# First token group of the last feed-forward block taken in two halves of 256 rows, late weight panels rounded on ScalarE

## The chip, the cores and the metric

The kernel runs on one core of a Trainium2 chip. The metric is the device time of one execution in microseconds (us), the median of three runs for the kernel before: 541.84 us (539.55 to 542.74). Lower is better.

## What is computed

Two batches of 1024 tokens of width 256 go through four residual blocks, all in float32: attention against 64 context rows per batch, a mixture of 16 experts of which each token takes two, a linear mix with a constant row of the context, and a feed-forward block with ternary weights. The change lies between the second and the fourth. Cut to that:

```
def _L1_xattn_ref(x1, x2, W, b):
    part1 = jnp.einsum('bld,ed->ble', x1, W1)
    part2 = jnp.einsum('bld,ed->be', x2, W2) / x2.shape[1]
    return part1 + part2[:, None, :] + b

def _L1_ffn_ref(x, w1_w, w1_s, w2_w, w2_s, h1_w, h1_s, h2_w, h2_s, w3_w, w3_s):
    h = jax.nn.silu(_tlin(x, w1_w, w1_s)) * _tlin(x, w2_w, w2_s)
    h = jax.nn.gelu(_tlin(h, h1_w, h1_s), approximate=False)
    h = jax.nn.gelu(_tlin(h, h2_w, h2_s), approximate=False)
    return _tlin(h, w3_w, w3_s)
...
x = x + tanh(g_ffn[0])   * L0_ffn(layernorm(x), ...)      # experts
x = x + tanh(g_xattn[1]) * L1_xattn(layernorm(x), ctx)    # linear mix
x = x + tanh(g_ffn[1])   * L1_ffn(layernorm(x), ...)      # 256 -> 1024 -> 1024 -> 1024 -> 256
```

## The kernel before

The 2048 tokens stand in X as 16 tiles of 128 rows, in NG = 4 groups of TG = 4 tiles (GN = 512 rows). Each engine has its own program, written out by hand in one order; engines meet only at semaphores. A matrix product in full float32 precision is made of products of the fp32r type: each operand is split in a rounded part (xTh, Ah, Bh, suffix h) and the rest (xTl, Al, Bl, suffix l). The ternary weights are exact in fp32r, so they need only the rounding copy from Wraw to Wr, in 44 panels of 512 columns; every product with them is two matmuls, one with the h part and one with the l part.

After the last of 47 expert blocks (NBLK) GpSimd (POOL) gathers the two expert rows of each token from ys_dram, `gather_rows` (L482 to L492): eight indirect DMAs for a group, into xn and y2. Then a group goes through this chain:

- VectorE (DVE) `x2` (L846): per tile two SCALAR_TENSOR_TENSOR into X (L850, L853), bn_stats (L859), bn_aggr (L861), at the end the variance into veps (L865).
- TensorE (PE) `T3` (L1411): two transposes a tile of X into banks 6 and 7. ScalarE (ACT) `high` (L1119) copies them to xTh, DVE `low3` (L867) makes xTl.
- POOL `root` (L439): rstd = veps ** -0.5; `add_row` (L494): adds the context row to the group's X.
- PE `part1` (L1422): three matmuls of 256 columns, twice, for each tile. DVE `x3` (L875): adds the product times rstd to X, then `statistics` (L544) for the fourth layer norm. POOL `root` again. DVE `normalise4` (L887): xn, one TENSOR_SCALAR a tile (L893). PE `T4` (L1432), ACT `high` (L1122), DVE `low4` (L896).
- `ffn` on all four engines (DVE L912, ACT L1124, PE L1439). Layer 1 has eight steps m (FK = 8): eight matmuls of 512 columns into two banks (L1468, L1471), banks alternating with m, so that step m waits for the DVE product of step m - 2 (semaphores f_h). ACT: Silu (L1134), then the copy to Ah (L1138). DVE: the product with the second bank (L917), then Al (L921). The layers h1 and h2 have eight steps of 16 matmuls of 512 columns (L1502, L1503) and Gelu on ACT (L1146); the last layer has 64 matmuls pairs of 256 columns (L1533, L1534).

For the groups 1 to 3 the chain is woven into the ffn of the group before, and hides there. For group 0 nothing is left to weave it into: it stands alone between the experts and the first ffn. PE fills that time with `keep_clock` (L1175), matmuls on the identity whose result nobody reads:

```
            eng.wait_ge(b_ye, NBLK)
            keep_clock(bank[0], 40)
            T3(0)
            keep_clock(bank[0], 8)
            part1(0)
            keep_clock(bank[0], 12)
            T4(0)
            keep_clock(bank[0], 4)
```

The panels are rounded by three engines: 0 to 7 on DVE among the expert blocks, 8 to 27 on ACT after them (L1116), and the last 16 (LATE) on POOL between its second root and the gathers of group 1 (L515). PE waits for the counters act_pan and pool_late before it uses a panel in group 0.

## Time and profile before

| | |
|---|---|
| median of 3 runs | 541.84 us (539.55 to 542.74) |
| the profiled execution | 541.48 us |
| its span in the profile | 539.7 us |
| mean granted TensorE clock | 0.961 of full |
| busy share: PE, DVE, ACT, POOL | 94%, 59%, 38%, 27% |

Times in the rows are in us from the start of the span. The profiled execution took 1.8 us more than its span, and 0.4 us less than the median. A matmul's duration includes the way through the array, so the step from one start to the next is the throughput; a matmul on float32 operands is recorded as two pieces. "Idle before" and an arrow name what ended the wait of that engine.

### The profile page before, as it was taken

The numbers are of one execution on the slowest core, as the hardware profiler recorded it, in microseconds if no ns is written. First come the engines' busy times: TensorE is split into PE (matmuls) and PEld (weight loads), VectorE is DVE, ScalarE is ACT, GpSimd is POOL, SyncE is SP. The second block draws the span as 40 slices with busy tenths as digits, with TensorE's granted clock in tenths as the row PEclk, the third lists the DMA queues.
The fourth block names the chain that finished last, engine by engine and source line by source line (L and its number), as shares of the span: only waits on it lengthen the run. The fifth ranks groups of instructions, "written<-read, shape, count | busy, mean of one in ns | idle before, by whom it ended". The sixth has DMA issues, their size and how long they took to land.

```text
span 539.7 us, 8120 instructions
## 1 busy us (share of the span) xinstructions
PE 509.5 (94%) x2866; PEld 435.1 (81%) x2866; DVE 320.6 (59%) x849; ACT 204.2 (38%) x453; POOL 148.0 (27%) x141
## 2 busy tenths in 40 slices
PE   8899998999998889999999999999999999999993
PEld 7778697888887767888897888897788888788883
DVE  3978956776652656874637775635686634644432
ACT  3666515666668035221226212224422123522120
POOL 1845336555525394110125020107011101000000
PEclk9778689999999799999999999999999999999998
DMA  8934214999883732231005031004122002022001
GB/s 291 310 101 135 67 41 118 316 302 311 223 144 91 279 105 65 57 80 40 1 1 156 21 97 60 0 2 136 40 78 72 7 1 79 1 79 78 21 1 44
DMA packets 33921, 54.63 MB, mean 101 GB/s; under 512 B 4081, under 2 KB 17905, under 8 KB 33874
## 3 DMA queue, kind: packets, MB, share of 16 engines
q1 hardware_dynamic: 29264, 43.06, 25.1%
q0 software_dynamic: 3792, 10.36, 8.2%
q10 hardware_dynamic: 818, 0.61, 0.4%
q8 instruction: 26, 0.43, 0.3%
q14 instruction: 21, 0.17, 0.1%
HBM read 43.66 MB, written 10.35 MB: 100 GB/s over the span
## 4 chain that ended last, share of the span: by engine, by line
PE 86%; DMA 4%; DVE 4%; issue 2%; POOL 2%; ACT 1%; SPq 0%; POOLq 0%; DVEq 0%
PE bank L1502 22%; PE bank L1503 22%; PE bank L1471 5%; PE bank L1468 5%; PE bank L1178 4%; PE bank L1171 4%; PE bank L1173 3%; PE bank L1172 3%; PE bank L1534 3%; PE bank L1533 3%; DMA xg<-xb_dram,perm 3%; PE bank L1361 2%; PE bank L1255 2%; PE bank L1231 2%; PE bank L1379 1%
## 5 line engine op out<-in xcount | busy, mean ns | idle before, releaser
L1146 ACT ACTIVATE sg<-bank,colv 128x512 f32<-128x512 f32 x64 | 44.1, 690 | 188.8 <-PE bank L1503 188.8
L1502 PE MATMUL bank<-Ah,Wr 128*128 128x512 f32 x256 | 100.2, 392 | 0.2 <-DVE sg L917 0.2
L1502 PE MATMUL bank<-Bh,Wr 128*128 128x512 f32 x256 | 99.9, 390 | 0.0
L1503 PE MATMUL bank<-Bl,Wr 128*128 128x512 f32 x256 | 99.7, 389 | 0.0
L1503 PE MATMUL bank<-Al,Wr 128*128 128x512 f32 x256 | 99.7, 389 | 0.0
L478 POOL DMA_INDIRECT xg<-xb_dram,perm x47 | 46.6, 991 | 42.9 <-PE bank L1361 21.3
L1502 PEld LDWEIGHTS bank<-Ah,Wr 128*128 128x128 f32 x256 | 48.0, 188 | 11.5 <-DVE sg L917 1.0
L1502 PEld LDWEIGHTS bank<-Bh,Wr 128*128 128x128 f32 x256 | 48.1, 188 | 9.8
L1503 PEld LDWEIGHTS bank<-Bl,Wr 128*128 128x128 f32 x256 | 48.1, 188 | 9.8
L1503 PEld LDWEIGHTS bank<-Al,Wr 128*128 128x128 f32 x256 | 48.1, 188 | 9.7
L930 DVE CAST Ah<-sg 128x512 fp32r<-128x512 f32 x32 | 13.6, 426 | 63.0 <-ACT sg L1146 63.0
L1471 PE MATMUL bank<-xTl,Wr 128*128 128x512 f32 x128 | 50.4, 394 | 0.2 <-DVE xTl L899 0.2
L1468 PE MATMUL bank<-xTh,Wr 128*128 128x512 f32 x128 | 50.4, 394 | 0.0
L441 POOL TENSOR_TENSOR rstd<-veps,mhalf 128x4 f32<-128x4 f32 x8 | 10.5, 1310 | 120.5 <-DVE veps L566 66.5
L917 DVE SCALAR_TENSOR_TENSOR sg<-bank,colv,sg 128x512 f32<-128x512 f32 x32 | 24.0, 751 | 24.2 <-ACT sg L1134 20.6
L1134 ACT ACTIVATE sg<-bank,colv 128x512 f32<-128x512 f32 x32 | 22.1, 689 | 42.1 <-PE bank L1471 37.7
L1178 PE MATMUL bank<-ident 128*128 128x128 f32 x252 | 35.3, 303 | 0.5 <-ACT yb L1100 0.5
L1178 PEld LDWEIGHTS bank<-ident 128*128 128x128 f32 x252 | 33.8, 216 | 2.2 <-issue 1.3
L930 DVE CAST Bh<-sg 128x512 fp32r<-128x512 f32 x32 | 13.6, 426 | 35.3 <-ACT sg L1146 35.3
L1171 PE MATMUL bank<-EL,bxh 128*128 x94 | 30.8, 327 | 1.2 <-DVE bxl L806 0.7
L1534 PE MATMUL bank<-Wr,Al 128*128 128x256 f32 x128 | 30.9, 283 | 0.0
L1533 PE MATMUL bank<-Wr,Ah 128*128 128x256 f32 x128 | 30.9, 283 | 0.0
(215 smaller groups left out, 1039.7 us busy)
## 6 DMA issues: line engine op xcount, KB each, us to landing
Wraw<-panels SPq DMA_DIRECT2D x22, 512.0 KB
stage<-panels SPq DMA_DIRECT2D x44, 256.0 KB
ES<-experts SPq DMA_DIRECT2D x16, 384.0 KB, 6.1
ys_dram<-yb SPq DMA_DIRECT2D x47, 128.0 KB
xb_dram<-xb SPq DMA_DIRECT2D x4, 512.0 KB, 4.0
X<-x SPq DMA_DIRECT2D x3, 512.0 KB, 7.6
out<-outb SPq DMA_DIRECT2D x3, 512.0 KB
xg<-xb_dram,perm POOLq DMA_INDIRECT x47
```

What stands on the lines that cost most here:

```text
L478: eng.indirect_dma_start(out=xg[:, i % 4, :], out_offset=None, in_=xb_dram, in_offset=bass.IndirectOffsetOnAxis(ap=perm[:, i:i + 1], axis= ...
L917: eng.scalar_tensor_tensor(sg[:, m % 3, :], bank[2 * (m % 2) + 1][:, :], colv[:, C_S2 + m:C_S2 + m + 1], sg[:, m % 3, :], ALU.mult, ALU.mu ...
L930: own(eng.tensor_copy(h[0][:, m, :], sg[:, r, :]))
L1146: eng.activation(sg[:, (8 * layer + m) % 3, :], bank[m % 4][:, :], ACT.Gelu, scale=colv[:, c + m:c + m + 1]).then_inc(f_act[m], 1)
L1171: mm(dst, lhs[0], rhs[1], start=first, stop=False)
L1178: mm(dst[:, 0:P], ident[:, :], ident[:, :], start=True, stop=True)
L1468: mm(dst, w[:, u, k, :], xTh[:, k, :], start=k == 0, stop=False)
L1471: ins = mm(dst, w[:, u, k, :], xTl[:, k, :], start=False, stop=k == DK - 1 and not general)
L1502: mm(bank[m % 4][:, :], Wr[:, base:base + P], h[0][:, k, :], start=k == 0, stop=False)
L1503: ins = mm(bank[m % 4][:, :], Wr[:, base:base + P], h[1][:, k, :], start=False, stop=k == FK - 1 and not general)
L1533: mm(dst, hA[0][:, k, j * P:(j + 1) * P], w, start=k == 0, stop=False)
L1534: ins = mm(dst, hA[1][:, k, j * P:(j + 1) * P], w, start=False, stop=k == FK - 1)
```

## The change

Group 0 goes through the chain, and through layer 1 of its ffn, in two halves of 256 rows (HN): `early` is rows 0 to 255, `late` rows 256 to 511. Every engine gets half versions of the functions (`root_half`, `add_row_half`, `x2_row`, `variance_half`, `low_half`, `x3_half`, `normalise4_half`, `high_half`, `T3_half`, `part1_half`, `T4_half`) and a function `early_layer1`: layer 1 for the early rows, with the second half's steps at fixed places in it. `ffn(0)` then makes layer 1 for the late rows only (`ts`), and the layers h1, h2 and w3 as before on 512 rows. The half versions use banks 4 and 5 for the product of part 1. Both halves of layer 1 have all eight steps, with matmuls of 256 columns: 128 matmuls where there were 64. The last 16 panels go from POOL to ACT: two after each Gelu of layer h1 of group 0. `keep_clock` in this place has 50 matmuls in all where it had 64. The groups 1 to 3 keep their code; only the semaphore counts are shifted by one (`passed(g)` = g + 2). The branch for weights that aren't exact is not taken.

```
@@ gpsimd @@
             gather_rows(0)
-            root(2, 0)
-            add_row(0)
-            root(3, 0)
-            for w in range(NPAN - LATE, NPAN):
-                raw_there(eng, w)
-                to, raw = panel(w)
-                eng.tensor_copy(to, raw).then_inc(pool_late, 1)
+            root_half(2, 0)
+            add_row_half(0)
+            root_half(3, 0)
+            root_half(2, 1)
+            add_row_half(1)
+            root_half(3, 1)
             for g in range(NG - 1):
                 gather_rows(g + 1)
@@ vector @@
+            def early_layer1():
+                for m in range(FK + 1):
+                    if m < FK:
+                        eng.wait_ge(e_act, m + 1)
+                        eng.scalar_tensor_tensor(sg[:, m % 3, early], bank[2 * (m % 2) + 1][:, early],
+                                                 colv[:, C_S2 + m:C_S2 + m + 1], sg[:, m % 3, early],
+                                                 ALU.mult, ALU.mult).then_inc(e_h, 1)
+                    if m > 0:
+                        eng.wait_ge(e_hh, m)
+                        eng.tensor_tensor(hA[1][:, m - 1, early], sg[:, (m - 1) % 3, early],
+                                          hA[0][:, m - 1, early].bitcast(F32), ALU.subtract).then_inc(e_hl, 1)
+                    if m == 1:
+                        x3_half(1)
+                    if m == 3:
+                        normalise4_half(1)
+                    if m == 6:
+                        low_half(1, n_h4, n_l4)
...
-            x2(0)
-            low3(0)
-            x3(0)
-            normalise4(0)
-            low4(0)
+            for j in range(2):
+                x2_row(0, j)
+            variance_half(2, 0)
+            low_half(0, n_h3, n_l3)
+            x2_row(0, 2)
+            x3_half(0)
+            x2_row(0, 3)
+            variance_half(2, 1)
+            normalise4_half(0)
+            low_half(1, n_h3, n_l3)
+            low_half(0, n_h4, n_l4)
+            early_layer1()
@@ scalar @@
+            def early_layer1():
+                for m in range(FK + 1):
+                    if m < FK:
+                        eng.wait_ge(e_pe, m + 1)
+                        if m >= 3:
+                            eng.wait_ge(e_hl, m - 2)
+                        eng.activation(sg[:, m % 3, early], bank[2 * (m % 2)][:, early], ACT.Silu,
+                                       scale=colv[:, C_S1 + m:C_S1 + m + 1]).then_inc(e_act, 1)
+                    if m > 0:
+                        eng.wait_ge(e_h, m)
+                        eng.activation(hA[0][:, m - 1, early], sg[:, (m - 1) % 3, early], ACT.Copy).then_inc(e_hh, 1)
+                    if m == 6:
+                        high_half(1, n_T4, n_h4)
...
+                        if g == 0 and layer == 1:
+                            w = NPAN - LATE + LATE // FK * m
+                            round_panels(w, w + LATE // FK)
@@ tensor @@
+            def early_layer1():
+                for m in range(FK):
+                    if m == 0:
+                        eng.wait_ge(n_h4, 1)
+                        eng.wait_ge(n_l4, 1)
+                    if m >= 2:
+                        eng.wait_ge(e_h, m - 1)
+                    eng.wait_ge(dve_pan, m + 1)
...
+                    if m == 0:
+                        part1_half(1)
+                    if m == 5:
+                        T4_half(1)
...
+                    elif g == 0:
+                        eng.wait_ge(n_h4, DK)
+                        eng.wait_ge(e_h, FK - 1 + m)
...
-            keep_clock(bank[0], 40)
-            T3(0)
-            keep_clock(bank[0], 8)
-            part1(0)
-            keep_clock(bank[0], 12)
-            T4(0)
-            keep_clock(bank[0], 4)
+            keep_clock(bank[0], 30)
+            T3_half(0)
+            keep_clock(bank[0], 3)
+            part1_half(0)
+            T3_half(1)
+            keep_clock(bank[0], 6)
+            T4_half(0)
+            keep_clock(bank[0], 3)
+            early_layer1()
```

How the instructions stand on VectorE, from the third tile of group 0 (L850 before, L867 now) to the first step of layer 1. Before, all of the chain comes ahead of the ffn's first product (L917):

```order
L850 SCALAR_TENSOR_TENSOR X<-xn,wtop,X 128x256
L853 SCALAR_TENSOR_TENSOR X<-y_60,wtop,X 128x256
L859 BN_STATS stats<-X 128x6
L861 BN_AGGR mv<-stats 128x2
L865 TENSOR_SCALAR veps<-mv 128x4
L870 TENSOR_TENSOR xTl<-bank,xTh 128x512 x2
L882 SCALAR_TENSOR_TENSOR X<-bank,rstd,X 128x256 x2
```

Now, from `low_half(0, n_h3, n_l3)` on:

```order
L892 TENSOR_TENSOR xTl<-bank,xTh 128x2x256
L867 SCALAR_TENSOR_TENSOR X<-xn,wtop,X 128x256
L870 SCALAR_TENSOR_TENSOR X<-y_60,wtop,X 128x256
L873 BN_STATS stats<-X 128x6
L875 BN_AGGR mv<-stats 128x2
L900 SCALAR_TENSOR_TENSOR X<-bank,rstd,X 128x256 x2
L904 BN_STATS stats<-X 128x6 x2
L907 BN_AGGR mv<-stats 128x2 x2
L887 TENSOR_SCALAR veps<-mv 128x2
L867 SCALAR_TENSOR_TENSOR X<-xn,wtop,X 128x256
```

The third tile now stands behind the first half's xTl, and the fourth tile behind the first half's `x3_half(0)`.

Further on in the same queue, the first steps of `early_layer1` (L964 is its product, L969 its Al):

```order
L964 SCALAR_TENSOR_TENSOR sg<-bank,colv,sg 128x256 x2
L969 TENSOR_TENSOR Al<-sg,Ah 128x256
L900 SCALAR_TENSOR_TENSOR X<-bank,rstd,X 128x256 x2
L904 BN_STATS stats<-X 128x6 x2
L907 BN_AGGR mv<-stats 128x2 x2
L887 TENSOR_SCALAR veps<-mv 128x2
L964 SCALAR_TENSOR_TENSOR sg<-bank,colv,sg 128x256
```

The product of step 2 stands behind the second half's `x3_half(1)`.

TensorE at the same place, from the first filler matmuls (L1281 is `keep_clock`) to the second half of part 1's first rows (L1520 is `T3_half`, L1537 `T4_half`):

```order
L1275 MATMUL bank<-W1h,xTl 128x256
L1276 MATMUL bank<-W1h,xTh 128x256
L1520 MATMUL bank<-ident,X 128x128 x4
L1281 MATMUL bank<-ident 128x128 x6
L1537 MATMUL bank<-ident,xn 128x128 x4
L1281 MATMUL bank<-ident 128x128 x3
L1553 MATMUL bank<-xTh,Wr 128x256
```

The transposes of the tiles 2 and 3 (four at L1520) now lie between the first half of part 1 and the first half of T4, with no filler between the two tiles.

## Rows read from the trace of the kernel before

**Rows 1.** The page: busy time, and the chain that ended last, by engine.
```profile
PE 509.5 (94%) x2866; PEld 435.1 (81%) x2866; DVE 320.6 (59%) x849; ACT 204.2 (38%) x453; POOL 148.0 (27%) x141
...
PE 86%; DMA 4%; DVE 4%; issue 2%; POOL 2%; ACT 1%; SPq 0%; POOLq 0%; DVEq 0%
```

**Rows 2.** Busy time by stretch: PE, PEld, DVE, ACT, POOL, then granted clock, DMA.
```profile
173.00:176.40 3.40, 0.80 (x6) 0.32 (x4) 2.04 (x6) 1.28 (x3) 2.52 (x3) 1.00 0.40 117
176.40:183.30 6.90, 4.96 (x22) 4.56 (x23) 4.04 (x10) 1.08 (x2) 3.35 (x2) 0.51 0.64 211
183.30:193.50 10.20, 7.96 (x64) 7.05 (x62) 6.19 (x18) 0.66 (x2) 4.80 (x9) 1.00 0.91 333
193.50:209.00 15.50, 15.34 (x67) 11.61 (x67) 9.72 (x15) 8.37 (x14) 13.20 (x18) 1.00 0.18 52
```

**Rows 3.** TensorE in order of time: start, us, what, idle time before it.
```profile
163.94 9.20 PE L1178 MATMUL bank<-ident 128*128 128x128 f32 x80 [0.47 <-ACT yb L1100]
...
179.51 3.62 PE L1178 MATMUL bank<-ident 128*128 128x128 f32 x16
...
183.45 0.28 PE L1171 MATMUL bank<-W1l,xTh 128*128 128x256 f32 x1
...
185.84 0.28 PE L1173 MATMUL bank<-W1h,xTh 128*128 128x256 f32 x1
...
193.58 0.47 PE L1468 MATMUL bank<-xTh,Wr 128*128 128x512 f32 x1
...
208.98 0.40 PE L1502 MATMUL bank<-Ah,Wr 128*128 128x512 f32 x1
```

**Rows 4.** VectorE in order of time, 174 to 200 us.
```profile
174.22 0.48 DVE L850 SCALAR_TENSOR_TENSOR X<-xn,wtop,X 128x256 f32<-128x256 f32 x1 [2.01 <-issue]
...
177.97 0.48 DVE L850 SCALAR_TENSOR_TENSOR X<-xn,wtop,X 128x256 f32<-128x256 f32 x1 [0.49 <-DMA y<-ys_dram,slots]
...
180.38 1.29 DVE L870 TENSOR_TENSOR xTl<-bank,xTh 128x512 fp32r<-128x512 f32 x2 [0.53 <-ACT xTh L1122]
184.82 0.88 DVE L882 SCALAR_TENSOR_TENSOR X<-bank,rstd,X 128x256 f32<-128x256 f32 x2 [3.15 <-PE bank L1173]
...
188.47 0.17 DVE L566 TENSOR_SCALAR veps<-mv 128x4 f32<-128x4 f32 x1
189.77 2.54 DVE L893 TENSOR_SCALAR xn<-X,mv,rstd 128x256 f32<-128x256 f32 x4 [1.13 <-POOL rstd L441]
...
197.00 0.75 DVE L917 SCALAR_TENSOR_TENSOR sg<-bank,colv,sg 128x512 f32<-128x512 f32 x1 [2.24 <-ACT sg L1134]
...
199.49 0.68 DVE L921 TENSOR_TENSOR Al<-sg,Ah 128x512 fp32r<-128x512 f32 x1
```

**Rows 5.** GpSimd in order of time, 179 to 199 us.
```profile
179.94 1.04 POOL L441 TENSOR_TENSOR rstd<-veps,mhalf 128x4 f32<-128x4 f32 x1 [3.81 <-DVE veps L865]
180.98 2.35 POOL L498 TENSOR_TENSOR X<-X,crow 128x1024 f32<-128x1024 f32 x1
...
189.71 9.24 POOL L515 CAST Wr<-Wraw 128x512 fp32r<-128x512 f32 x16
```

**Rows 6.** ScalarE in order of time.
```profile
159.10 0.39 ACT L1084 ACTIVATE bxh<-bank 128x256 fp32r<-128x256 f32 x1
...
163.79 10.49 ACT L1116 ACTIVATE Wr<-Wraw 128x512 fp32r<-128x512 f32 x20
...
196.28 0.69 ACT L1134 ACTIVATE sg<-bank,colv 128x512 f32<-128x512 f32 x1 [2.35 <-PE bank L1471]
...
216.52 0.69 ACT L1146 ACTIVATE sg<-bank,colv 128x512 f32<-128x512 f32 x1 [2.95 <-PE bank L1503]
```

**Rows 7.** VectorE in order of time, inside the ffn of group 0.
```profile
235.84 2.77 DVE L932 TENSOR_TENSOR Bl<-sg,Bh 128x512 fp32r<-128x512 f32 x1
...
259.92 1.38 DVE L893 TENSOR_SCALAR xn<-X,mv,rstd 128x256 f32<-128x256 f32 x4
```

**Rows 8.** GpSimd in order of time, inside the ffn of group 0.
```profile
235.58 2.48 POOL L498 TENSOR_TENSOR X<-X,crow 128x1024 f32<-128x1024 f32 x1 [9.17 <-PE bank L1418]
```

More of the change, by code:

```diff
@@ L311, in panel, with passed @@
             return Wr[:, w * PANEL:(w + 1) * PANEL], Wraw[:, w * PANEL:(w + 1) * PANEL]
+        HN = GN // 2
+        early, late = slice(0, HN), slice(HN, GN)
+        def passed(g):
+            return g + 2
         def tiles(g):
@@ new lines, in low_half, with x3_half @@
+            def low_half(h, ready, done_sem):
+                eng.wait_ge(ready, h + 1)
+                ts = slice(h * HN, (h + 1) * HN)
+                eng.tensor_tensor(xTl[:, :, ts], bank[6 + h][:, :].rearrange("p (k t) -> p k t", k=DK),
+                                  xTh[:, :, ts].bitcast(F32), ALU.subtract).then_inc(done_sem, 1)
+            def x3_half(h):
+                eng.wait_ge(n_row, h + 1)
+                eng.wait_ge(ln_rstd[2], h + 1)
+                eng.wait_ge(n_p1, h + 1)
+                for j in range(2 * h, 2 * h + 2):
+                    own(eng.scalar_tensor_tensor(tiles(0)(j), bank[4 + h][:, (j % 2) * D:(j % 2 + 1) * D],
+                                                 rstd[:, 2, j:j + 1], tiles(0)(j), ALU.mult, ALU.add))
+                own.done()
+                for j in range(2 * h, 2 * h + 2):
+                    own(eng.bn_stats(stats[:, j, :], tiles(0)(j)))
+                own.done()
+                for j in range(2 * h, 2 * h + 2):
+                    own(eng.bn_aggr(mv[:, 3, j, :], stats[:, j, :]))
+                variance_half(3, h)
@@ L867, in low3, with normalise4_half @@
+            def normalise4_half(h):
+                eng.wait_ge(ln_rstd[3], h + 1)
+                for j in range(2 * h, 2 * h + 2):
+                    eng.tensor_scalar(xn[:, j, :], tiles(0)(j), mv[:, 3, j, 0:1], rstd[:, 3, j:j + 1],
+                                      ALU.subtract, ALU.mult).then_inc(n_xn, 1)
             def low3(g):
@@ L1408, in _, with T3_half @@
                     load_offsets(i + 2)
+            def T3_half(h):
+                for j in range(2 * h, 2 * h + 2):
+                    if j == 1:
+                        keep_clock(bank[0], 8)
+                    eng.wait_ge(n_x2, j + 1)
+                    for k in range(DK):
+                        ins = eng.transpose(bank[6 + h][:, k * HN + (j % 2) * P:k * HN + (j % 2 + 1) * P],
+                                            tiles(0)(j)[:, k * P:(k + 1) * P], ident[:, :])
+                ins.then_inc(n_T, 1)
@@ new lines, in early_layer1 @@
+            def early_layer1():
[6 more added lines that the diff above has]
+                    eng.wait_ge(dve_pan, m + 1)
+                    w = Wr[:, m * PANEL:(m + 1) * PANEL].rearrange("p (u k n) -> p u k n", u=2, k=DK)
+                    for u in range(2):
+                        dst = bank[2 * (m % 2) + u][:, early]
+                        for k in range(DK):
+                            mm(dst, w[:, u, k, :], xTh[:, k, early], start=k == 0, stop=False)
+                            ins = mm(dst, w[:, u, k, :], xTl[:, k, early], start=False, stop=k == DK - 1)
+                    ins.then_inc(e_pe, 1)
+                    if m == 0:
+                        part1_half(1)
+                    if m == 5:
+                        T4_half(1)
```

140 lines of the change are left out of this document (85 added, 55 removed).

## The prediction

> **What bounds the kernel now.** The page comes first: PE is busy for 94% of the span and makes up 86% of the chain that ended last [rows 1]. That is an average over two kinds of stage, so I took the time apart by stretch. From 193.5 us on PE is busy all the time [rows 2], and it stays so to the end but for the last store: what happens after layer 1 of group 0 has begun costs exactly PE's own work. Between the end of the experts and that point PE does little that is wanted. It runs fillers from 163.94, and the first matmul of layer 1 starts at 193.58 [rows 3]. These 29.6 us are a chain through all engines: gathers, x2, transposes, xTl, part 1, x3, root, normalise, transposes, xTl. The reader should see two marks there: 193.58, where layer 1 starts, and 208.98, where layer h1 starts [rows 3]. From 208.98 on, the two kernels have the same PE work, so **the whole question is whether the first matmul of h1 comes before or after 208.98**. I walk the new order through, engine by engine, with durations from the rows.
>
> **Prices.** A matmul of 256 columns takes 0.12 us from start to start: 20 steps between 183.45 and 185.84 [rows 3]. A step of layer 1 for half the rows (eight of them) is 0.96, where the whole one is (208.98 - 193.58) / 8 = 1.92. So PE pays nothing or 0.2 us for splitting; the first step before had short waits in it. ACT on 256 columns takes 0.39 against 0.69 on 512 [rows 6]. DVE on 256 columns from PSUM or from SBUF takes 0.48, on 512 0.75 [rows 4]; for Al on 256 columns I take 0.41, between half of 0.68 and 0.48. A half of xTl or xTh is one instruction of 512 elements, 0.65 [rows 4]. From the last matmul's start to the next engine's is 0.3 us, and 0.03 to 0.1 for the other hand-overs. POOL's root is 1.04 whatever its size (bounds 0.5 and 1.4), the added row for half the group half of 2.35, 1.2 [rows 5].
>
> **Until layer 1 starts for the early rows.** The rows of tile 1 are on DVE at 174.22 [rows 4], and the gathers are untouched. X is there at 175.2, transposed at 175.8, xTh at 176.4, xTl at 177.1; part 1 (12 matmuls) runs from 177.2 to 178.8. POOL's root starts at 176.25, its added row runs from 177.3 to 178.5. DVE takes tile 2 from 177.06. Its two operations read two SBUF tiles each, and the second would start at 177.58, under POOL's addition. What that costs no row shows for this operation; the nearest one is the TENSOR_TENSOR at 235.84, 2.77 us where the same operation on Al takes 0.68 [rows 4]: it ends just after POOL's addition of 235.58 [rows 7, 8]. So an operation with two SBUF inputs has waited for POOL there. Bounds: nothing, or the rest of the addition, 1.15 us; I take the latter. Tile 2 is then through at 179.8, `x3_half(0)` takes 2.3 us (for four tiles it was 184.82 to 188.64 [rows 4]), tile 3 1.75, its variance 0.17: 183.9. Normalising two tiles takes 0.7: the four took 2.54 while POOL was casting panels [rows 4, 5], and 1.38 where it wasn't [rows 7]. That is the one sure gain of taking the casts off POOL, 0.6 us a half. `keep_clock(6)` after the transposes of tile 3 (183.1 to 183.4) ends at 184.85, so T4 starts then; xTh at 186.3, xTl at 187.0: **layer 1 starts at 187.05, 6.5 us before 193.58**.
>
> The Trainium skill (SBUF — State Buffer, Who interferes with whom) states that a VectorE instruction with two SBUF inputs and a GpSimd one that reads SBUF exclude each other for a whole instruction. That covers SCALAR_TENSOR_TENSOR too, which no row here shows; by it the 1.15 us are owed, without it the start is 186.05.
>
> **The early layer.** Its 64 matmuls are 7.7 us, part 1 of the late rows 1.44, T4 0.6. PE would be done in 9.7. DVE isn't: eight products and eight Al are 7.1 us, and x3 (2.3), normalise (0.7) and xTl (0.65) of the late rows stand among them in its queue, 10.8 in all, before any wait. Steps 0 to 3 of PE run from 187.05 to 192.6. The product of step 2 stands behind `x3_half(1)`, which ends at 194.0, so PE's step 4 waits for it until 194.55: **2.0 us idle**. Steps 4 and 5, T4 and steps 6 and 7 then run to 199.0. The late rows' xTh stands on ACT behind Silu 6 and copy 5, their xTl on DVE behind the product of step 6 and an Al: ready at 200.2, so PE idles 1.1 us more and starts the late half at 200.3. Early part: 13.2 us where PE's work is 9.7.
>
> **The late half.** Two steps in flight, as before, but with half the work against the same hand-overs: from the end of step m to the start of m + 2 it takes 0.17 (way through the array) + 0.04 + 0.39 + 0.04 + 0.48 + 0.07 = 1.19 us, and step m + 1 covers 0.96 of it. So two steps cost 2.15 where the 512-row form had all of this covered (1.92 us against some 1.7). Eight steps: 8.4 us, to 208.7. The Al of step 7 is needed only at the fifteenth matmul of h1, 3.2 us later, and is there.
>
> **Sum of the steps:** 208.7 against 208.98, -0.3 us. Layer 1 starts 6.5 us earlier, but where it took 15.4 us in one piece it now takes 13.2 + 8.4 = 21.6, 6.2 more: 2.0 is chain work of the late rows that PE does inside it, 3.1 are the two holes, and the rest are the longer steps.
>
> **The clock.** Before, PE ran at 1.2 GHz from 176.4 to 183.3 (granted 0.51) and at 2.4 GHz afterwards [rows 2]; it had been busy for 0.80 of the 3.4 us ahead of the fall. It cost little, for what PE did then was filler (16 pieces in 3.62 us against 80 in 9.20 [rows 3]). Now the holes are: 1.4 us at 173.9, 3.6 us between the transposes of tiles 2 and 3, 2.0 in the early layer. A fall behind the second doubles the 2.2 us of PE work between tile 3's transposes and layer 1, and perhaps a step or two. I put in 0.9 us, between nothing (fall at the old place) and 2.2 (a stretch as long as the old one that begins at 183.3).
>
> **The panels.** ACT's 16 copies are 0.52 each [rows 6], 1.05 after each Gelu of h1, where ACT idles 2.95 [rows 6]. The panels landed before POOL cast them, by 198.95 [rows 5]; the first use is the third step of h2. Cost nothing; were the cover gone, 8.4 us. The gathers of group 1 start at about 196.5, where they came behind POOL's last cast; their rows are first read after the second step of h1. On SP nothing is moved.
>
> **Forecast:** +0.6 us. On the profiled execution that is 541.48 + 0.6; the median was 0.36 above it: 542.4 us. What three runs can tell from no change is about 0.5%, 2.7 us: this forecast says no difference.
>
> **Rivals.**
> 1. *The clock falls where it hurts* (the other side). Mechanism: PE is idle for 3.6 us before tile 3, the clock is at 1.2 GHz at 183.3 to 190, so T3, fillers, T4, step 0 and part 1 of the late rows run at half speed (+2.2); the 2 us hole behind step 3 and the one at 199 bring a second fall, where the late steps take 1.8 instead of 0.96 while it lasts (+0.8 to 1.5). Together 211.2 to 212.6, +2.2 to +3.6: 544.0 to 545.5. It decides over 0.5% when both falls come. For it: the old fall came after less idle time than this. Against: the fall before was over by the time it could cost. Chance 0.25, 0.16 of it over the bound.
> 2. *The detours hide.* POOL's addition doesn't stop DVE (-1.0), hand-overs and 256-column operations are shorter than I took them: 207.0 to 207.7, -1.3 to -2.0: 539.8 to 540.5. If DVE's detour cost PE nothing at all, PE would need 17.4 us from 186.05, h1 at 203.5, -5.5: 536.3. Against: `x3_half(1)` stands ahead of the product that PE waits for, in one queue. Chance 0.24, 0.11 of it over the bound.
> 3. *The panels aren't hidden on ACT*, so a Gelu comes late: 8.4 us at most, 550. Against: the 2.95 us holes. Chance 0.02.
> The forecast keeps 0.49.
>
> **Range:** 539.6 to 545.0: rival 2's reachable part and most of rival 1; left out are the full gain of rival 2, the end of rival 1 and rival 3. Faster by over 0.5% 0.11, within 0.71, slower 0.18.
>
> **What the profile should show.** Right: first matmul of layer 1 at 186 to 188.5, a hole of about 2 us before its fifth step put down to DVE, another of about 1 us before the late half, late steps 1.05 to 1.1 us apart, h1 at 208.5 to 210.5, ACT's 16 copies in h1 without a hole on PE, DVE's tile 2 held for 1 us by POOL. Wrong: h1 before 207 (the DVE queue isn't what holds the early layer), or beyond 211.5 (clock or a wait that I haven't seen), or any new idle time of PE after h1 has begun.

## The result, and the profile after

The changed kernel takes **552.2 us** (median of 4 runs, 550.3 to 554.9) where the kernel before, on the same chip, takes 542.29 (4 runs): ratio 1.0197, 95% interval 1.0162 to 1.0231. It is 10 us slower, where I forecast 0.6 and a range up to 545.0. The profiled execution took 551.5 us, with a span of 549.7.

The page after, the lines that answer to [rows 1]:

```profile
PE 513.6 (93%) x2902; PEld 442.2 (80%) x2902; DVE 321.4 (58%) x867; ACT 214.8 (39%) x485; POOL 140.4 (26%) x128
...
PE 84%; DMA 4%; DVE 3%; ACT 3%; issue 2%; another core or an unknown queue 2%; POOL 0%; ACTq 0%; DVEq 0%
```

The new item in the chain is "another core or an unknown queue 2%". This program runs on one core, so these are waits for which the profile has found no releaser. They are three pieces, 8.5 us together, of a loss of some 10. The chain in order of time:

```profile
176.17 3.54 another core or an unknown queue
...
208.45 2.88 another core or an unknown queue
...
212.13 2.06 another core or an unknown queue
```

TensorE in order of time, changed kernel (L1281 is filler, L1520 the transposes of X, L1553 the early layer, L1618 and L1621 the late half, L1649 h1):

```profile
175.89 0.44 PE L1520 MATMUL bank<-ident,X 128*128 128x128 f32 x2 [0.19 <-issue]
176.16 0.83 PE L1281 MATMUL bank<-ident 128*128 128x128 f32 x6
181.10 0.38 PE L1274 MATMUL bank<-W1l,xTh 128*128 128x256 f32 x1 [4.11 <-DVE xTl L892]
...
192.49 0.36 PE L1553 MATMUL bank<-xTh,Wr 128*128 128x256 f32 x1 [0.36 <-issue]
...
204.86 0.38 PE L1618 MATMUL bank<-xTh,Wr 128*128 128x256 f32 x1 [0.41 <-ACT xTh L1199]
...
212.40 0.58 PE L1618 MATMUL bank<-xTh,Wr 128*128 128x256 f32 x1 [2.46 <-issue]
...
215.26 0.58 PE L1618 MATMUL bank<-xTh,Wr 128*128 128x256 f32 x1 [0.79 <-DVE sg L984]
...
220.13 0.50 PE L1649 MATMUL bank<-Ah,Wr 128*128 128x512 f32 x1
```

h1 starts at 220.13, where [rows 3] have 208.98. Behind it the kernels are alike: 549.7 - 220.13 = 329.6 us against 539.7 - 208.98 = 330.7.

The expert stage ahead, whose code is the same, ends at another time in each execution, so from here on I count from **the issue of the first gather of group 0 on POOL**: 166.42 in before, 168.31 after. That row moved between 164.2 and 169.0 over all kernels below. From it to h1 before takes 42.56 us and the changed kernel 51.82: **9.26 us are to be explained**, all of them in this stretch.

Engines meet at semaphores, counters that an instruction raises when it is done and for which another engine waits. On PE the last transpose of a half raises n_T, and the last matmul of a step of layer 1 raises f_pe. ScalarE in order of time, changed kernel, shows who is late (L1199 is xTh, L1232 the late half's Silu):

```profile
179.73 0.60 ACT L1199 ACTIVATE xTh<-bank 128x512 fp32r<-128x512 f32 x1 [3.56 <-remote]
...
206.72 0.47 ACT L1232 ACTIVATE sg<-bank,colv 128x256 f32<-128x256 f32 x1 [0.34 <-PE bank L1621]
207.67 0.48 ACT L1232 ACTIVATE sg<-bank,colv 128x256 f32<-128x256 f32 x1 [0.48 <-PE bank L1621]
...
211.35 0.47 ACT L1232 ACTIVATE sg<-bank,colv 128x256 f32<-128x256 f32 x1 [2.90 <-remote]
...
214.21 0.47 ACT L1232 ACTIVATE sg<-bank,colv 128x256 f32<-128x256 f32 x1 [2.09 <-remote]
```

The transposes for which xTh waits end at 176.33 (175.89 + 0.44). ACT had been idle for 3.56 us and yet starts at 179.73. The trace also records when a semaphore goes up: n_T, which the last of these transposes raises, does so at 179.71, **3.4 us after its matmul**. POOL's added row, which waits for the same semaphore, starts at 179.78. In the late half the steps 2 and 3 end at 208.99 and 209.94; their semaphores go up at 211.32 and 214.19, **2.3 and 4.25 us late**. All other updates of PE from 176 to 220 us are within 0.02 us of the matmul's end. What was under way meanwhile, POOL in order of time (each line an indirect gather of 128 rows; the first and last of group 0 and of group 1, six between them each time):

```profile
168.31 0.95 POOL L504 DMA_INDIRECT xn<-ys_dram,slots  x1 [13.39 <-DMA ys_dram<-yb]
...
177.09 0.95 POOL L504 DMA_INDIRECT y<-ys_dram,slots  x1 [0.30 <-issue]
...
202.84 1.02 POOL L504 DMA_INDIRECT xn<-ys_dram,slots  x1 [2.56 <-PE bank L1537]
...
211.72 0.95 POOL L504 DMA_INDIRECT y<-ys_dram,slots  x1 [0.30 <-issue]
```

The packets of the last gather of group 0 arrive up to 179.52, those of group 1's last up to 214.12: both times the last held update comes just behind (179.71 and 214.19). And the clock, by stretch, with the columns of [rows 2]:

```profile
176.40:183.30 6.90, 2.79 (x18) 2.60 (x16) 2.52 (x7) 0.60 (x1) 3.34 (x4) 0.87 0.42 139
183.30:193.50 10.20, 7.02 (x36) 6.45 (x36) 5.62 (x16) 1.19 (x2) 2.90 (x3) 0.58 1.05 392
193.50:205.00 11.50, 9.40 (x75) 8.79 (x73) 7.93 (x23) 5.95 (x15) 2.56 (x3) 1.00 0.07 21
205.00:212.40 7.40, 4.46 (x33) 3.86 (x33) 3.53 (x9) 2.93 (x8) 5.57 (x7) 0.99 0.35 104
212.40:220.10 7.70, 6.89 (x32) 6.39 (x32) 3.14 (x9) 3.01 (x8) 0.27 (x1) 0.56 0.09 27
```

Behind each stall comes a stretch near 1.2 GHz. The second (0.56) falls on steps 4 to 7 of the late half, which are wanted work.

The kernel before has the same burst of gathers beside the same short fillers, and loses nothing there. Between 166.42, its first gather, and 179.72, the end of tile 3's transposes, PE has no semaphore to raise. Its one n_T goes up at 179.73, when the gathers are in. The half versions put a hand-over from PE into the middle of the burst.

### The profile page after: what moved, and what is told of

It is laid out like the page before. It is cut to its first block, busy times and chain, and to the rows that moved or that the text cites. A ratio compares the mean times of both kernels' runs of the same rounds, so it can differ in the third digit from the quotient of the medians.

```text
span 549.7 us, 8235 instructions
## 1 busy us (share of the span) xinstructions
PE 513.6 (93%) x2902; PEld 442.2 (80%) x2902; DVE 321.4 (58%) x867; ACT 214.8 (39%) x485; POOL 140.4 (26%) x128
## 4 chain that ended last, share of the span: by engine, by line
PE 84%; DMA 4%; DVE 3%; ACT 3%; issue 2%; another core or an unknown queue 2%; POOL 0%; ACTq 0%; DVEq 0%
PE bank L1649 21%; PE bank L1650 21%; PE bank L1618 5%; PE bank L1621 5%; PE bank L1281 4%; PE bank L1274 3%; DMA xg<-xb_dram,perm 3%; PE bank L1276 3%; PE bank L1681 3%; PE bank L1680 3%; PE bank L1275 3%; ACT Wr L1192 2%; PE bank L1464 2%; PE bank L1358 2%; PE bank L1334 2%
## 5 line engine op out<-in xcount | busy, mean ns | idle before, releaser
L1244 ACT ACTIVATE sg<-bank,colv 128x512 f32<-128x512 f32 x64 | 44.1, 690 | 181.1 <-PE bank L1650 181.1
L1649 PE MATMUL bank<-Ah,Wr 128*128 128x512 f32 x256 | 100.3, 392 | 0.1
L1649 PE MATMUL bank<-Bh,Wr 128*128 128x512 f32 x256 | 99.9, 390 | 0.0
L1649 PEld LDWEIGHTS bank<-Ah,Wr 128*128 128x128 f32 x256 | 48.1, 188 | 11.1 <-DVE Al L988 0.7
L1649 PEld LDWEIGHTS bank<-Bh,Wr 128*128 128x128 f32 x256 | 48.1, 188 | 9.8
L1618 PE MATMUL bank<-xTh,Wr 128*128 128x512 f32 (+1 forms) x128 | 48.3, 383 | 3.8 <-issue 2.5
L1621 PE MATMUL bank<-xTl,Wr 128*128 128x512 f32 (+1 forms) x128 | 47.6, 378 | 0.3 <-issue 0.3
L456 POOL TENSOR_TENSOR rstd<-veps,mhalf 128x4 f32<-128x4 f32 x6 | 8.4, 1401 | 117.9 <-DVE veps L585 61.1
L1232 ACT ACTIVATE sg<-bank,colv 128x512 f32<-128x512 f32 (+1 forms) x32 | 20.3, 636 | 43.3 <-PE bank L1621 34.5
L984 DVE SCALAR_TENSOR_TENSOR sg<-bank,colv,sg 128x512 f32<-128x512 f32 (+1 forms) x32 | 21.9, 684 | 26.3 <-ACT sg L1232 21.0
L1618 PEld LDWEIGHTS bank<-xTh,Wr 128*128 128x128 f32 x128 | 25.8, 202 | 10.6 <-issue 2.8
L1281 PE MATMUL bank<-ident 128*128 128x128 f32 x224 | 33.4, 312 | 0.5 <-ACT yb L1175 0.5
L1281 PEld LDWEIGHTS bank<-ident 128*128 128x128 f32 x224 | 31.9, 226 | 2.2 <-issue 1.3
```

The source lines that it names most:

```text
L984: eng.scalar_tensor_tensor(sg[:, m % 3, ts], bank[2 * (m % 2) + 1][:, ts], colv[:, C_S2 + m:C_S2 + m + 1], sg[:, m % 3, ts], ALU.mult, ALU ...
L1232: eng.activation(sg[:, m % 3, ts], bank[2 * (m % 2)][:, ts], ACT.Silu, scale=colv[:, C_S1 + m:C_S1 + m + 1]).then_inc(f_act[m], 1)
L1244: eng.activation(sg[:, (8 * layer + m) % 3, :], bank[m % 4][:, :], ACT.Gelu, scale=colv[:, c + m:c + m + 1]).then_inc(f_act[m], 1)
L1281: mm(dst[:, 0:P], ident[:, :], ident[:, :], start=True, stop=True)
L1618: mm(dst, w[:, u, k, :], xTh[:, k, ts], start=k == 0, stop=False)
L1621: ins = mm(dst, w[:, u, k, :], xTl[:, k, ts], start=False, stop=k == DK - 1 and not general)
```

## The experiments

Theories. **G**: PE's semaphore updates are held back while POOL's indirect gathers are in flight. **F**: PE's own instruction fetch holds them (a fetch stood near both places, at 176.8 and 207.2). **I**: they are held while PE has nothing to do. **N**, formed after the runs up to p4_latefill: it takes both, several gathers in a row and short PE instructions at full rate. Times compare with the runs of before on the same chip.

### e1_act_panels: the panels on ACT alone

```diff
-            for w in range(NPAN - LATE, NPAN):      # POOL, ahead of the gathers of group 1
...
-                eng.tensor_copy(to, raw).then_inc(pool_late, 1)
...
+                        if g == 0 and layer == 1:   # ACT, two panels after each Gelu of h1
...
+                                eng.activation(to, raw, ACT.Copy).then_inc(act_pan, 1)
```

> The kernel before with one part of the change alone: the 16 late panels are rounded on ACT after each Gelu of h1 and not on POOL. All theories of the slowdown (clock, late semaphore updates) expect the time of before within 1 us, since ACT idles 2.9 us per step of h1 there, or up to 1 us less, because normalising for layer 4 isn't slowed by POOL's casts. If the panels were the cause, +5 us or more.

Measured: 543.65 us against 544.19, ratio 0.9997 (0.9959 to 1.0036). The panels cost nothing. (Without the casts POOL issued group 1's gathers at 194.07, 5 us earlier than before, and two updates in layer 1 came 1.3 and 0.9 us late: the first sign that 512-column matmuls aren't wholly safe either.)

### e2_gather_late: the gathers of group 1 held

```diff
+                if g == 1:
+                    eng.wait_ge(f_h[FK - 1], 1)
                 for j in range(TG):
```

> The changed kernel, with POOL's gathers of group 1 held until the last product of layer 1 of group 0 is there. Theory G (PE's semaphore updates are held back while POOL's indirect gathers are landing): the two late updates between 209 and 215 us (2.3 and 4.2 us late) are gone, with them the second stretch at 1.2 GHz; h1 starts 6 to 8 us earlier, 544 to 546 us; the first late update (at 176 to 180) stays. Theory F (PE's instruction fetch holds them): both stay, 552 us.

Measured: 546.97 us against 544.19, ratio 1.0049 (1.001 to 1.0088). Every update of the late half is on time, and it runs at 2.4 GHz, from 204.83 to 214.65, 9.82 us, where the changed kernel took 220.13 - 204.86 = 15.27. h1 comes 46.92 us after the first gather: **the second place is worth 4.9 us**. The first late update stays (3.6 us).

### e3_shift: PE's fetches moved by 64 instructions

```diff
-                    keep_clock(bank[5], 30)
+                    keep_clock(bank[5], 14)
```

> The changed kernel with 64 fewer filler matmuls on PE ahead of the experts (keep_clock 14 for 30), so that PE's instruction fetches fall 64 instructions later in the program. Theory F (the fetch holds the updates): the late updates at 176 and 209 move or vanish, h1 starts over 3 us earlier. Theory G (gathers): both late updates stay, each at the landing of the last gather of its group; 552 us within 2.

Measured: 552.3 us, ratio 1.016 (1.0099 to 1.0221). The fetch of 176.8 now comes at 188.2, and the update is late all the same, by 3.6 us; the later two by 2.5 and 4.4. Each update goes up at nearly the same distance from its group's first gather as in the changed kernel (11.5 us for the first, 11.40 there; 8.6 and 11.5 for the later two, 8.5 and 11.35 there). **F has fallen.**

### e4_busy: 13 more fillers behind the transposes

```diff
-            keep_clock(bank[0], 3)
+            keep_clock(bank[0], 16)
             part1_half(0)
```

> The changed kernel with 52 more filler matmuls behind the transposes of tiles 0 and 1 (keep_clock 16 for 3), so that PE isn't idle while it waits for their xTl. Theory I (updates are held only while PE has nothing to do): ACT's xTh starts within 0.5 us of the transposes' end, part 1 about 3 us earlier than now but behind the fillers; no first stretch at 1.2 GHz, h1 3 to 8 us earlier. Theories G and F: the update still comes only with the last landing of the gathers (at 179.7), but PE is at 2.4 GHz behind it; h1 1 to 3 us earlier.

Measured: 552.31 us, ratio 1.0152 (1.0095 to 1.021). **I has fallen**: PE had fillers to issue, and the update still came 3.5 us late. (The total is as before the edit, but h1 came 50.3 us after the first gather, 1.5 earlier than in the changed kernel, since PE was at 2.4 GHz behind the stall.) More than that, PE itself stopped inside the fillers, with nothing to wait for. TensorE in order of time:

```profile
174.70 1.39 PE L1281 MATMUL bank<-ident 128*128 128x128 f32 x11
177.54 0.38 PE L1281 MATMUL bank<-ident 128*128 128x128 f32 x2 [1.45 <-issue]
178.26 2.28 PE L1281 MATMUL bank<-ident 128*128 128x128 f32 x19 [0.33 <-issue]
```

A fetch of PE's instructions (175.5 to 176.7) may account for the first of the two gaps, not for the second.

### p1_probe: an increment on every second filler

```diff
+            def probed(dst, n):
+                for i in range(n):
+                    ins = mm(dst[:, 0:P], ident[:, :], ident[:, :], start=True, stop=True)
+                    if i % 2:
+                        ins.then_inc(probe, 1)
```

> A probe of when PE's semaphore updates are late: the changed kernel with an increment of an otherwise unused semaphore on every second filler matmul ahead of, between and behind the transposes of tiles 0 and 1, and 16 fillers for 3 behind them. Theory G (held as long as a gather is in flight, whatever PE does): all increments after the first landing at about 170.5 come late, some by microseconds. Theory I (held only while PE waits for something): all increments from the dense fillers are on time, within 0.05 us of the matmul's end. If the updates are on time to about 175 and late from there, it is the length of time or the number of gathers that have gone by which decides.

Measured: 549.27 us, one execution (before 539.64). The fillers' increments are due every 0.45 us. The times at which they went up, 27 in all (the first nine, on time, left out):

```
... 170.31 170.76 171.21 171.65 172.25 173.68 177.94 179.37 179.43 179.49 179.59 179.65 179.71 179.77 179.83 180.00 180.44 180.89
```

The first gather was issued at 168.04. Up to 171.65, with three gathers issued, all are on time. The next four were due at 172.09, 172.54, 173.99 and 174.44 and come 0.2, 1.1, 4.0 and 4.9 us late; and from 179.37, when the packets of the last gather have landed (up to 179.3), the backlog drains at one each 0.06 us. The transposes' own update, at 179.53, stands in this row in its turn. It is the updates that are late, not the matmuls: between 173.99 and 177.94, while that one update was due, PE started 28 later matmuls. That answers neither G nor I as they were stated: updates aren't held from the first gather on, they **fall behind and queue up**.

### p2_split: two tiles' gathers behind the transposes

```diff
-            gather_rows(0)
+            gather_rows(0, (0, 1))
             root_half(2, 0)
             add_row_half(0)
+            gather_rows(0, (2, 3))
```

> The changed kernel, with the gathers of tiles 2 and 3 of group 0 issued behind the added row of tiles 0 and 1, so that PE's transposes of tiles 0 and 1 end when no gather is under way. Theory G: their update is on time (at about 8 us after the first issue, not 11.5), part 1 of the early rows starts 3 us earlier; tiles 2 and 3 come 3 to 4 us later, so the total may be no better, 548 to 556 us. If the update is late all the same, the gathers aren't what holds it.

Measured: 551.17 us, ratio 1.0207 (1.0153 to 1.0261). ACT's xTh:

```profile
175.71 0.60 ACT L1200 ACTIVATE xTh<-bank 128x512 fp32r<-128x512 f32 x1 [0.23 <-PE bank L1521]
```

It starts 0.03 us after the transposes' end at 175.68. The four gathers issued up to 171.38 were in and the next was issued at 178.30: with no gather in flight the update is on time. The time is no better, since tiles 2 and 3 come later and the second place is untouched (2.3 and 4.3 us late again).

### p3_wide and p4_latefill: the late half with longer, and with more, matmuls

```diff
-                ts = slice(0, GN) if g else late          # p3_wide, on PE
+                ts = slice(0, GN)
```
```diff
                     ins.then_inc(f_pe[m], 1)              # p4_latefill
+                    if g == 0:
+                        keep_clock(bank[4], 2)
```

> The changed kernel, where PE computes all 512 columns again in the late half of layer 1 (the early 256 of them are not used): 1.92 us a step instead of 0.96, without waits, while the gathers of group 1 land as they do in the changed kernel. If short matmuls or PE's waits are a condition of the late updates, all f_pe updates are on time and h1 starts 15.4 to 15.8 us after the late half's first matmul, at about 220.5 and at 2.4 GHz; the total is 550 to 553 us. If gathers alone hold them, two updates are 2 to 4 us late, h1 starts beyond 223.

> The changed kernel with four filler matmuls (0.46 us) behind each step of the late half, so that PE hardly waits between the steps. Theory I (held only while PE waits): no update late, no second stretch at 1.2 GHz, late half about 11.5 us, h1 starts at 216 to 217, 3 us earlier than in the changed kernel. Theory G: the updates of steps 2 and 3 still 2 and 4 us late, h1 at 219 to 221.

Measured, one execution each: p3_wide 552.86 us, updates of steps 2 and 3 0.2 and 1.25 us late instead of 2.3 and 4.25, h1 at 221.65, with no stretch near 1.2 GHz in the late half. p4_latefill 551.29 us, updates of steps 1 to 3 late by 0.4, 3.3 and 3.5, h1 at 220.03. So filling PE's waits with short matmuls makes more updates late, and matmuls of twice the length make the lateness smaller. This is where I formed N; p3_wide's expectation had the direction right and "all on time" wrong.

### n1_nofill and n2_widefill: PE's instructions while group 0 is gathered

Both also hold the gathers of group 1, as e2_gather_late does, which is what they compare with.

```diff
-            keep_clock(bank[0], 30)                       # n1_nofill; and the 8 of T3_half
             T3_half(0)
```
```diff
+            def keep_clock_wide(n):                       # n2_widefill, for the 30 and the 8
+                for _ in range(n):
+                    mm(bank[0][:, :], Wr[:, 0:P], Wr[:, 0:PANEL], start=True, stop=True)
```

> The changed kernel with the gathers of group 1 held (as in e2_gather_late) and without the fillers ahead of and between the transposes of tiles 0 and 1, so that PE issues next to nothing while the gathers of group 0 land. Theory N (it takes both, gathers in flight and many short PE instructions; the updates queue up): the update of the transposes is on time, within 0.1 us, part 1 starts 3 us earlier, though PE may be at 1.2 GHz. Theory G (gathers alone): it comes 3.5 us late, 11.5 us after the first gather's issue, as in all runs so far.

> The changed kernel with the gathers of group 1 held and with fillers of 512 columns (one instruction of 0.24 us) in place of pairs of 128-column ones ahead of and between the transposes of tiles 0 and 1: the same PE time in half the instructions. Theory N: the transposes' update is late by less than 1 us, part 1 starts 2.5 to 3.5 us earlier, h1 follows by as much; 542 to 545 us. Theory G: late by 3.5 us, time as e2_gather_late, 547 us.

Measured: n1_nofill 541.53 us, one execution, against a median of 541.66. ACT's xTh starts at 174.86, 0.04 us after the transposes' end (174.13 + 0.69), with seven of the eight gathers issued: **gathers alone held nothing**. n2_widefill 542.46 us, ratio 1.0011 (0.9983 to 1.0038), update 0.5 us late; layer 1 starts 21.52 us after the first gather (24.72 in e2_gather_late), h1 43.72 after it (46.92). **The first place is worth 3.2 us.** Leaving out the fillers that were there to hold the clock did as well (h1 at 43.53), although PE was granted 0.50, 1.2 GHz, from 168 to 186 us.

With the update on time, DVE's tile 2 meets POOL's addition, as I had forecast and as it does not in the changed kernel. VectorE and POOL in order of time, n2_widefill:

```profile
174.86 0.69 DVE L894 TENSOR_TENSOR xTl<-bank,xTh 128x512 fp32r<-128x512 f32 x1 [0.72 <-issue]
175.47 2.25 DVE L869 SCALAR_TENSOR_TENSOR X<-xn,wtop,X 128x256 f32<-128x256 f32 x1
177.75 0.48 DVE L872 SCALAR_TENSOR_TENSOR X<-y,wtop,X 128x256 f32<-128x256 f32 x1
```
```profile
175.43 0.74 POOL L452 TENSOR_TENSOR rstd<-veps,mhalf 128x2 f32<-128x2 f32 x1
176.14 1.29 POOL L515 TENSOR_TENSOR X<-X,crow 128x512 f32<-128x512 f32 x1
```

The operation takes 2.25 us for 0.48 and ends 0.3 after POOL's addition.

### b1_pairs and b2_pairs_held: the same effect put into the kernel before

```diff
+                        if g == 0:                        # layer 1: two 256-column matmuls for one of 512
...
+                            for ts in (slice(0, GN // 2), slice(GN // 2, GN)):
+                                for k in range(DK):
+                                    mm(dst[:, ts], w[:, u, k, :], xTh[:, k, ts], start=k == 0, stop=False)
+                                    ins = mm(dst[:, ts], w[:, u, k, :], xTl[:, k, ts], start=False, stop=k == DK - 1)
```

b2_pairs_held adds the two lines of e2_gather_late.

> The kernel before, with each 512-column matmul of layer 1 of group 0 written as two of 256 columns: the same columns in twice the instructions, while the gathers of group 1 land behind steps 3 to 7. Theory N: f_pe updates become 1 to 4 us late there, PE waits and h1 starts 2 to 6 us later than before, 542 to 548 us. Theory I or any that needs the change's order: all on time, time of before within 1 us (540).

> Control for b1_pairs: the kernel before, layer 1 of group 0 in pairs of 256-column matmuls, and the gathers of group 1 held until its last product. Theory N: no update late, h1 42.5 to 43.5 us after the first gather's issue as in before (42.56), where b1_pairs had 48.5; time of before within 1 us. If the pairs themselves cost, 547 us as b1_pairs.

Measured, one execution each: b1_pairs 547.09 us (before 541.66, the slowest of its 16 runs 544.75), b2_pairs_held 540.12 (before 541.39). Layer 1, from its first matmul to h1's, takes 208.98 - 193.58 = 15.40 us in before [rows 3], 215.98 - 195.98 = 20.00 in b1_pairs, 208.62 - 193.19 = 15.43 in b2_pairs_held. ScalarE in order of time, b1_pairs:

```profile
203.93 0.69 ACT L1134 ACTIVATE sg<-bank,colv 128x512 f32<-128x512 f32 x1 [0.71 <-PE bank L1472]
204.52 0.62 ACT L1138 ACTIVATE Ah<-sg 128x512 fp32r<-128x512 f32 x1
208.61 0.69 ACT L1134 ACTIVATE sg<-bank,colv 128x512 f32<-128x512 f32 x1 [3.47 <-remote]
...
211.55 0.69 ACT L1134 ACTIVATE sg<-bank,colv 128x512 f32<-128x512 f32 x1 [1.73 <-remote]
```

In b1_pairs the updates of steps 4 and 5 are 2.8 and 3.8 us late; in b2_pairs_held none is, and in before, with 512 columns beside gathers too, ScalarE starts each step's Silu within 0.05 us of its last matmul's end. The same columns and the same number of increments in twice the instructions cost 4.6 us beside the gathers and nothing without them. **N is shown**, in a kernel that has nothing else of the change. (What b2_pairs_held missed is its 42.5 to 43.5: h1 came 44.42 after the first gather, since layer 1 itself began 1.8 us later than in before; that lies ahead of its edit.)

### c1_wideonly: the first place alone

The wide fillers of n2_widefill, the gathers of group 1 as in the change.

> The changed kernel with the 512-column fillers of n2_widefill alone; the gathers of group 1 are as in the change. If the two places add up: layer 1 starts as in n2_widefill (21.5 us after the first gather's issue), the two updates in the late half are still 2.3 and 4.3 us late, h1 starts 48 to 49 us after the first gather's issue (changed kernel 51.8, n2_widefill 43.7), 547 to 549 us. If the second stall depended on the first, h1 comes at 44 to 46.

Measured: 548.63 us, ratio 1.0111 (1.0056 to 1.0166). Updates 0.5 us late at the first place, 2.35 and 4.25 at the second; h1 48.85 us after the first gather. The two places add up:

| | group 1's gathers as in the change | held |
|---|---|---|
| short fillers | 51.82 (changed kernel) | 46.92 (e2) |
| wide fillers | 48.85 (c1) | 43.72 (n2) |

First gather to h1, us; before has 42.56. The first place is worth 3.0 to 3.2, the second 4.9 to 5.1, and 1.2 are left: the change without the stalls, but for 0.5 us of lateness that the wide fillers leave.

### s2_reorder and c2_best: can the two halves win?

s2_reorder: the early rows all the way to layer 1 first, tiles 2 and 3 gathered behind POOL's addition, the late rows' transposes and part 1 inside the early layer:

```diff
+            gather_rows(0, (2,))
             root_half(3, 0)
+            gather_rows(0, (3,))
...
+                    if m == 1:
+                        T3_half(1)
+                    if m == 3:
+                        part1_half(1)
```

> Meant to beat both kernels if N holds: as n2_widefill, and the gathers of tiles 2 and 3 of group 0 issued behind the added row of tiles 0 and 1; x3, normalising and transposes of the early rows go ahead of everything of the late rows, whose transposes, part 1 and x3 stand inside the early layer (after its steps 1, 3, 4). Theory N or G (updates on time because no gather is in flight): layer 1 starts at about 20 us after the expert stage's end instead of 26.6, h1 3 to 6 us earlier than in before; 535 to 539 us. If the late rows' chain (tile 3 lands 19 us after the first gather's issue) holds the late half: 539 to 543.

Measured: 545.78 us against 541.66, ratio 1.0067 (1.0033 to 1.01), where I had hoped for 535 to 543. All updates are on time. Layer 1 starts 17.2 us after the first gather, but PE then waits for the late rows' chain (1.35, 2.41 and 1.36 us), is granted 0.50 from 200 to 205, and h1 comes 47.4 us after the first gather. The early start was lost again because the rest couldn't follow.

c2_best, from n2_widefill:

```diff
-            add_row_half(0)                               # POOL; both halves now on DVE
...
             x2_row(0, 2)                                  # DVE
+            add_row_half(0)
             x3_half(0)
...
             low_half(0, n_h4, n_l4)
+            add_row_half(1)
+            x3_half(1)
             early_layer1()
...
+                    if j == 3:                            # PE, in T3_half
+                        keep_clock_wide(13)
...
-            keep_clock(bank[0], 6)
+            keep_clock_wide(4)
             T4_half(0)
-            keep_clock(bank[0], 3)
+            part1_half(1)                                 # was behind step 0 of the early layer
             early_layer1()
```

> From n2_widefill (512-column fillers, gathers of group 1 held): the added row on DVE and not on POOL, which stopped DVE's tile 2 for 1.8 us there; 512-column fillers between the transposes of tiles 2 and 3, where PE idled 3.2 us and its clock fell; part 1 and x3 of the late rows ahead of layer 1 and not inside it. Layer 1 starts 18.6 to 19.5 us after the first gather's issue (n2_widefill 21.5), h1 39.5 to 41.5 (before 42.56): 538.5 to 540.5 us where before is 541.7, ratio 0.994 to 0.998. If a new DVE hole of over 2 us opens at step 2 of the early layer, no better than before.

Measured: **537.86 us against 541.39, ratio 0.9927 (0.9903 to 0.9951)**. It beats the kernel before by 0.7% and the changed one by more. Busy time by stretch, with the granted clock third from the right:

```profile
165.00:175.00 10.00, 9.07 (x40) 7.15 (x40) 2.21 (x6) 10.00 (x20) 5.63 (x6) 1.00 0.29 90
175.00:185.00 10.00, 8.26 (x47) 6.18 (x45) 8.83 (x25) 1.95 (x5) 4.33 (x6) 1.00 0.58 190
185.00:195.00 10.00, 8.96 (x71) 8.55 (x72) 7.89 (x22) 5.38 (x13) 0.70 (x1) 1.00 0.88 325
195.00:206.00 11.00, 10.32 (x77) 9.19 (x75) 8.33 (x21) 7.29 (x20) 0.00 (x0) 1.00 0.00 1
```

The clock doesn't fall in any of these stretches. The added row takes DVE 0.66 us, and tile 2's operations are back at 0.48. Layer 1 starts 18.78 us after the first gather, h1 38.08 after it, 1.4 better than the low end expected. With x3 of the late rows ahead of layer 1, PE's longest hole inside it is 0.81 us, where n2_widefill has 1.56. Four edits went in together, so what each is worth isn't shown.

## Why the prediction was wrong, step by step

**What bounds.** Right: all of the difference lies before h1, which starts 11.15 us later while the rest is 1.1 us shorter; 1.89 of it is the expert stage's own spread.

**The failed step** is in "Prices": *"From the last matmul's start to the next engine's is 0.3 us"*. No row beside it has a burst of gathers that meets short matmuls, and I used it at two places where one does: "transposed at 175.8, xTh at 176.4", and the 1.19 us from step m to step m + 2 in the late half. There it was 3.7, 2.6 and 4.5 us. Beside it stand two sentences that costed the gathers at nothing: "the gathers are untouched" and, of group 1, "their rows are first read after the second step of h1". I asked when their data is needed, not what they do to others while they run. Halving the matmuls doubled PE's instructions per microsecond beside them, and I costed only its columns. Shown by the four cells of the table and by b1_pairs against b2_pairs_held.

**The trace of before had a hint.** In the expert stage PE runs 128-column matmuls beside gathers of its own, and updates are late there too. In before, the transpose of 93.00 and ACT's copy of its result:

```profile
93.00 0.27 PE L1379 MATMUL bank<-ident,bh 128*128 128x128 f32 x1
```
```profile
94.11 0.28 ACT L1093 ACTIVATE bhh<-bank 128x128 fp32r<-128x128 f32 x1 [0.46 <-PE bank L1379]
```

The matmul ends at 93.27, ACT is idle from 93.65 and starts 0.84 us after the matmul's end, where I had read 0.3 from the matmul's start. The releaser's name hides it: the wait is put down to PE, whose matmul was long through.

**Until layer 1.** Forecast 187.05, that is 20.63 us after the first gather. The changed kernel took 24.18. Without the stall (n2_widefill) it is 21.52, 0.9 late, and the parts differ more than their sum. Tile 1 was on DVE 6.5 us after the first gather, where I had taken over the 7.8 of before (174.22). It is 7.6 to 7.9 in the traces of before, e1 and the two b kernels and 6.5 in the changed kernel and seven variants of it; why isn't known. That was 1.3 us in the change's favour. POOL held DVE's tile 2 for 1.8 us, not 1.15, since the root ahead of the addition counted too. Even so tile 3's transposes came 16.25 us after the first gather, forecast 16.7. From there to layer 1 it took 5.27 us, forecast 3.95: T3, fillers and T4 ran at 1.2 GHz, which the forecast had in its separate term of 0.9.

The Trainium skill (SBUF — State Buffer, Who interferes with whom) says that the two engines exclude each other for whole instructions. The trace of n2_widefill agrees as far as VectorE waits for POOL (2.25 us for 0.48), and in c2_best, where the addition is off POOL, the operation is back at 0.48. In the changed kernel itself the two hardly met, because the addition was late as well. (187.05 less the 1.15 us is 185.90, not the 186.05 of the prediction.)

**The early layer.** Forecast 13.2 us with holes of 2.0 and 1.1; measured 204.86 - 192.49 = 12.4, with holes of 1.56, at the forecast place, and 0.41. Mechanism right, holes too large by 0.4 and 0.7 us.

**The late half.** Forecast 8.4 us; without the stalls 9.8 (e2, n2). Of it, 0.7 are the wait for xTl behind the first matmul, the rest steps of (209.42 - 200.33) / 8 = 1.14 us instead of 1.07. In the changed kernel 15.3.

**The sum.** Forecast +0.6 us. n2_widefill, the change without the stalls, has a ratio of 1.0011, +0.6 us on 541.66, with an interval of 0.9983 to 1.0038. That agreement is partly luck: the late half was 1.4 too short, the early layer 0.8 too long, the start 0.9 early, against a clock term of 0.9 put in by judgement, and by its own trace h1 of n2_widefill is 1.2 us later than in before.

**The clock, rival 1.** Half right. In n2_widefill, with no stall to speak of, PE idled 3.22 us ahead of tile 3's transposes and was granted 0.67 from 182 to 187, as rival 1 has it. In the changed kernel T3 of tile 3, fillers and T4 ran at 1.2 GHz too, and so did steps 4 to 7 of the late half. But the second fall came behind the second stall, not behind the holes that I had named; in n2_widefill, which has these, it doesn't come. From 212.40 to 220.13 the last four steps took 7.7 us, where at 1.14 they take 4.6: with the 0.79 us hole among them, I estimate that 2.4 of the second place's 5.0 us are the clock. (Rival 1's own sum is uneven: 208.7 + 2.2 + 0.8 to 1.5 is 211.7 to 212.4, not 211.2 to 212.6.)

**Panels, normalising.** Right: 16 panels on ACT in pairs of 1.14 us (forecast 1.05), no hole on PE, e1 at 0.9997. Normalising a half takes 0.73, forecast 0.7.

**What would show it wrong.** The text named h1 "beyond 211.5 (clock or a wait that I haven't seen)". It was a wait, and then the clock.

## What to carry to other kernels

Splitting work into halves to start sooner halves the instructions too: where a burst of indirect gathers runs beside them, read what PE's semaphores do, not only what its columns cost, and move the burst to a stretch of long matmuls. Fillers that hold the clock are instructions like any others; long ones hold it with half as many, and here the short ones cost 3 us in a stretch where they were meant to help. A hand-over time read in one stretch may not hold in another, as here (0.3 against 2.6 to 4.5 us); a wait put down to "remote" on a single core, or to an engine that had long finished, should be cleared up before any edit is costed.

## What the runs showed of the hardware that I had not expected

PE's semaphore updates fell behind its matmuls by up to 4.9 us while indirect gathers were issued back to back (one each 1.25 us, landing 2.5 us after issue) and PE issued pairs of weight load and matmul every 0.11 to 0.12 us. From the probe: on time for the first 3.6 us of the burst, then a growing queue, drained at one each 0.06 us once the last gather has landed (179.37 on). With PE at a pair each 0.24 us the lateness is 0 to 1.3 us; with PE nearly idle (n1_nofill) ScalarE starts 0.04 us after the matmul's end. Plain transfers didn't do it: in c2_best the queues move some 390 GB/s from 185 to 193 us while PE issues 256-column matmuls for most of the time, and each of the seven updates in that stretch is on time within 0.02 us. What inside the chip holds the updates isn't known from these runs, nor whether it is the gathers' descriptors or their packets; that wasn't tried. How much the expert stage, where updates are late too, loses by it wasn't tried either.
